# Four-layer gated transformer on one core: the 8-dim-head attentions move from bf16 stacks to fp32 slots of 64 rows, filled by copies

## What is computed

```python
scores = jnp.einsum('bqhd,bkhd->bhqk', qh, kh) / jnp.sqrt(dh)
attn = jax.nn.softmax(scores + mask, axis=-1)
ctx = jnp.einsum('bhqk,bkhd->bqhd', attn, vh)
```

## Time and profile before

| what | value |
|---|---|
| time, median of 3 executions | 2059.91 us |
| lowest, highest | 2056.92, 2062.85 us |
| the profiled execution | 2044.2 us |
| its span | 2042.4 us |
| mean granted TensorE clock | 0.862 |
| instructions | 34774 |
| busy PE, DVE, ACT, POOL | 1367.1, 1399.3, 806.4, 450.7 us |

### The profile page before, as it was taken

The page is one execution under the profiler, slowest core; times in us unless marked ns, Lnnn a source line. Parts: engine busy times, 40 slices in busy tenths (PEclk is TensorE's granted clock), DMA queues, the critical chain, the costliest instruction groups (busy, mean ns, idle before and its releaser), DMA issues. The chain is left out here.

```text
span 2042.4 us, 34774 instructions
## 1 busy us (share of the span) xinstructions
PE 1367.1 (67%) x13754; PEld 958.2 (47%) x13754; DVE 1399.3 (69%) x2126; ACT 806.4 (39%) x1151; POOL 450.7 (22%) x598
## 2 busy tenths in 40 slices
PE   0788169999999933888888731588323777130898
PEld 0465146666666621565565511466213444120797
DVE  5566447777777767677767688466685775859565
ACT  0466137776677731333333220366220676010110
POOL 6421342222222100222222103332004230000221
PEclk9999669999999976999999855699766799555898
DMA  2011322222222201000000000000000000110242
GB/s 67 1 10 10 93 63 86 87 90 87 82 92 87 87 31 33 1 1 1 1 1 1 1 11 23 1 2 2 11 10 21 1 2 1 61 21 0 88 142 87
DMA packets 97737, 76.52 MB, mean 37 GB/s; under 512 B 42612, under 2 KB 84148, under 8 KB 96692
## 3 DMA queue, kind: packets, MB, share of 16 engines
q1 hardware_dynamic: 96564, 73.10, 12.0%
q0 software_dynamic: 1024, 1.32, 0.3%
HBM read 33.10 MB, written 3.15 MB: 18 GB/s over the span
## 5 line engine op out<-in xcount | busy, mean ns | idle before, releaser
L1088 DVE TENSOR_REDUCE Mf<-bank 128x4 f32<-128x1024 f32 x192 | 234.5, 1221 | 107.4 <-PE bank L974 107.4
L551 ACT ACTIVATE Pt<-bank 128x768 f32<-128x768 f32 (+1 forms) x192 | 169.4, 882 | 135.5 <-PE bank L492 134.8
L1041 ACT ACTIVATE Pt<-bank 128x1024 f32<-128x1024 f32 x192 | 196.9, 1025 | 50.8 <-PE bank L992 50.3
L1314 POOL TENSOR_TENSOR Psum<-Pt 128x512 f32<-128x512 f32 x64 | 81.1, 1267 | 313.7 <-ACT Pt L1433 313.7
L761 PE MATMUL bank<-ident,Qf 128*128 128x128 f32 x64 | 14.3, 416 | 159.5 <-SPq L262 96.1
L1481 DVE RECIPROCAL st<-bank 128x256 f32<-128x256 f32 x64 | 111.9, 1748 | 6.5 <-PE bank L1394 6.4
L992 PE MATMUL bank<-QK 50*128 50x256 f32 x768 | 97.6, 333 | 19.4 <-DMA QK<-NMrow 19.0
L576 DVE TENSOR_REDUCE Mx<-bank 128x2 f32<-128x256 f32 x128 | 54.3, 424 | 81.6 <-PE bank L479 77.6
L1456 DVE TENSOR_TENSOR qk_lo<-bank,qk_hi 128x512 fp32r<-128x512 f32 x64 | 44.1, 689 | 95.6 <-ACT qk_hi L1425 95.6
L898 POOL CAST parts<-nodes 128x256 fp32r<-128x256 f32 x96 | 38.2, 397 | 304.7 <-PE bank L954 304.7
L1005 PE MATMUL bank<-Pt,V 128*32 128x256 f32 x1536 | 103.5, 387 | 0.1
(11 more groups left out here) (367 smaller groups left out, 3691.9 us busy)
## 6 DMA issues: line engine op xcount, KB each, us to landing
QK<-Z SPq DMA_DIRECT2D x288, 128.0 KB, 3.1
Wup<-in_L_upT SPq DMA_DIRECT2D x16, 512.0 KB, 3.5
Wdn<-in_L_downT SPq DMA_DIRECT2D x16, 256.0 KB, 3.7
Aup<-in_L_aupT SPq DMA_DIRECT2D x16, 128.0 KB, 3.5
QK<-NMrow SPq DMA_DIRECT2D x96, 4.0 KB
WeT<-in_L_WeT SPq DMA_DIRECT2D x1, 1280.0 KB
s_rows<-XG SPq DMA_DIRECT2D x1, 1032.0 KB, 7.9
tA<-in_x_heads SPq DMA_DIRECT2D x1, 1024.0 KB
```

The costliest lines, as they stand in the source:

```text
L551: act.activation(Pp[:, g % 4, :, 0:w], banks[:, 2:4, 0:w], ACT.Exp, scale=L.scale).then_inc(exp_done, 1)
L1041: act.activation(Pp[:, g % 4], banks[:, 2:4, :], ACT.Exp, scale=L.scale).then_inc(exp_done, 1)
L1088: d.tensor_reduce(m, banks[:, 0:2, :].rearrange("p h (t k) -> p h t k", t=2), AX, ALU.max).then_inc(max_done, 1)
L1314: e.tensor_tensor(Psum[:, q % 2], Pp[:, q % 4, :, 0:S], Pp[:, q % 4, :, S:2 * S], ALU.add).then_inc(key_sum, 1)
```

## The change

The class `Heads` and its functions for each engine are removed, and l0x, l2x and l3x become a `Flow` as well. A slot has 64 rows in all of them, of which A uses 63 and B all 64. The three copies of a row stand at a distance of 64/dh rows (8 for dh 8, 4 for dh 16) where l0f had 3. Row 3 of a slot (`PAD`) takes the padding mask, row 63 (`TOP`) the negated maximum. The ring of `QK` has 4 places in l0f and 3 in the others, which need 8 blocks of two slots where l0f needs 4.

What a batch of the three attentions does for its slots now, in the order of the letters in `events()`: **S**, POOL permutes q and k into `order` with four copies (L379), PE turns them with four fp32 transposes (L468), ACT copies the bank into `Z`; **L**, DVE subtracts (L653); **D**, six DMAs of 128 KB (L368) on SP, and one more in l2x for the padding mask; **N** twice per batch, two small transposes each (L514), `NMrow` (L641) and a DMA of 8 KB (L355). A is L505, B is L528, V is L545, R is L554. Masks, exp and the order A, B, V stay as they were in these attentions; l0f keeps its own order, B before A.

Around it: the blank rows are now filled by POOL for the queries (`queries_blank`, L336) and by ACT for the keys (`keys_blank`), in l0f too, where POOL had all eight; ones are written into V (`values_ones`) at each attention, and V is cleared in l0x alone; `padf` becomes `padr`, 16 by 2048, computed on POOL (L1583).

```diff
-class Heads:
-    ...
-        def att_pool(g, L, base, pad=None, early=False):
...
-                e.tensor_copy(C[:, :, 5:6], k)
-                g.link(e.tensor_copy(C[:, :, 0:4:3], wide(k, 2)))
-                g.link(e.tensor_tensor(rk, k, C[:, :, 0:1], ALU.subtract))
...
+SLOT, PAD, TOP = 64, 3, 63
...
+        self.blocks = self.H // 2
+        self.half = self.blocks // 2
+        self.step = SLOT // dh
+        self.copies = 6 + padded
+        self.ring = 4 if node else 3
...
-                if ok(b):
+                if ok(b) and self.node:
                     out.append(("B", b, j))
                 if ok(a):
                     out.append(("A", a, j))
+                if ok(b) and not self.node:
+                    out.append(("B", b, j))
...
+                elif not self.node and j == 0 and ok(w):
+                    out.append(("L", w, 0))
...
+                elif not self.node and j in (1, 3) and ok(w):
+                    out.append(("D", w, j // 2))
...
+        def queries_blank(g, L):
+            for r in range(L.ring):
+                g.eng.tensor_copy(L.QK[:, r, :, 0, :], bc(L.rowk[:, 0:1].unsqueeze(1), [P, L.blocks, S]))
+        def keys_blank(a, L):
+            for r in range(L.ring):
+                a.eng.copy(L.QK[:, r, :, 1, :], bc(L.rowk[:, 1:2].unsqueeze(1), [P, L.blocks, S]))
...
+                    if L.padded and j == 0:
+                        e.dma_start(L.QK[PAD:P:SLOT, u % L.ring, :, 1, :].bitcast(F32),
+                                    padr[:, u, :].bitcast(F32)).then_inc(L.slots_in[u % L.ring], 16)
+                    rows = slice(SLOT * j, SLOT * (j + 1))
                     for f, pick in enumerate((slice(1, 3), slice(1, 4, 2), slice(0, 3, 2))):
-                        o = L.slot * j + f
-                        e.dma_start(QK[o:o + 3 * L.dh:3, u % L.ring].bitcast(F32),
-                                    Z[rows, u % 2, pick, :].bitcast(F32)).then_inc(slots_in[u % L.ring], 16)
+                        e.dma_start(L.QK[SLOT * j + f:SLOT * (j + 1):L.step, u % L.ring].bitcast(F32),
+                                    L.Z[rows, u % 2, pick, :].bitcast(F32)).then_inc(L.slots_in[u % L.ring], 16)
...
+                if kind == "S" and not L.node:
+                    for k, src in enumerate((Qf, Kf)):
+                        for t in range(2):
+                            e.tensor_copy(L.permuted(L.order[:, u % 2, k, t, :], out=True),
+                                          L.permuted(src[:, 2 * u + t, :])).then_inc(L.parts_in, 1)
...
+                    if L.causal:
+                        mask_a(g)
+                        after, m, o = events[i + 1]
+                        if after == "B":
+                            mask_b(Pb + L.pairs * m + o)
...
+                            rs = slice(SLOT * x, SLOT * x + TOP)
+                            last = pe.matmul(bank[x][:, t * S:t * S + w],
+                                             L.QK[rs, u % L.ring, j, 0, t * P:(t + 1) * P],
+                                             L.QK[rs, u % L.ring, j, 1, 0:w], start=(not L.causal and t == 0),
+                                             stop=True, skip_group_check=True)
...
+                    else:
+                        last = act.copy(L.Z[:, u % 2, 1:3, :].rearrange("p k s -> p (k s)"), b)
...
+                    else:
+                        last = d.tensor_tensor(L.Z[:, u % 2, 0:4:3, :], b.rearrange("p (k s) -> p k s", k=2),
+                                               L.Z[:, u % 2, 1:3, :].bitcast(F32), ALU.subtract)
```

More of the change, by code:

```diff
@@ L145, in events @@
                         out.append(("O", b, 0))
-                if j == 1 and ok(z):
+                if j == (1 if self.node else self.pairs - 1) and ok(z):
                     out.append(("S", z, 0))
@@ L192, in flamingo @@
         Mx = sb("Mx", [P, 2, 16])
+        L0 = Flow("l0x", 8, True, B)
+        L0f = Flow("l0f", 16, False, 6 * B, node=True)
+        L2 = Flow("l2x", 8, True, B, padded=True)
+        L3 = Flow("l3x", 8, False, B)
+        attentions = [L0, L0f, L2, L3]
         Rden = sb("Rden", [P, 2, 16])
@@ L402, in att_steps @@
[L402 to L409 removed]
+        bases, pb_, ub_ = [], 0, 0
+        for L in attentions:
+            bases.append({"P": pb_, "U": ub_})
+            pb_, ub_ = pb_ + L.units * L.pairs, ub_ + L.units * L.outs
+        t_full, t_done, u_full, u_done = sem("t_full"), sem("t_done"), sem("u_full"), sem("u_done")
+        y_full, y_done = sem("y_full"), sem("y_done")
+        wd_in, w_full, w_hi, w_done = sem("wd_in"), sem("w_full"), sem("w_hi"), sem("w_done")
@@ L532, in turn_bank @@
[L532 to L547 removed]
+                    b = turning(kind, u, j)
@@ L548, in att_act, with flow_act @@
+        def flow_act(a, L, base):
+            act = a.eng
+            Pb, Ub = base["P"], base["U"]
+            place = L.banks()
+            for kind, u, j in L.events():
+                g = Pb + L.pairs * u + j
+                c, n = u // B, u % B
+                if kind == "B":
                     act.wait_ge(st_full, g + 1)
@@ L573, in att_dve, with flow_dve @@
+        def flow_dve(v, L, base):
+            d = v.eng
+            Pb, Ub = base["P"], base["U"]
+            place = L.banks()
+            for kind, u, j in L.events():
+                g = Pb + L.pairs * u + j
+                c, n = u // B, u % B
+                if kind == "A":
                     d.wait_ge(sm_full, g + 1)
-                    hs = slice(2 * i, 2 * i + 2)
+                    m = L.Mf[:, u % 2, j // L.half, :, 0:2 * L.half].rearrange("p t (r i) -> p r t i", r=2)
+                    m = m[:, :, :, j % L.half]
```

854 lines of the change are left out of this document (300 added, 554 removed).

## The result

| kernel | median | lowest, highest | runs |
|---|---|---|---|
| before | 2061.05 us | 2054.68, 2069.89 | 20 |
| changed | 2067.59 us | 2058.61, 2087.04 | 20 |

The ratio is 1.0038 with a 95% interval of [1.0021, 1.0055]: the change makes the kernel slower by about 8 us (the two medians lie 6.5 us apart). Measured once more on another occasion it was 1.0040 [1.0016, 1.0063]. The profiled execution took 2071.8 us, its span 2069.8. The profiled execution of before (2044.2) was an unusually short one: none of the 20 runs reached it, and another profile of the same kernel has a span of 2058.2.

A forecast was written before the change was run, and what follows sets the result against it. No engine is full; chains (rings of DVE maxima and PE scores, plus turns) bound it. Terms -20 +1.2 +3.1 +5.5 -4.2 +1.0 +0.7 +2.4 = -10.3 from 2044.2 give 2033.9, scaled to 2049.5 us; range 2032 to 2071.

The forecast's parts named there:

- An l3x batch is 15.4: Steady l3x batch: 8 x 1.81 + 0.9 us instead of 17.26; over 7 batches -13 us.
- A causal batch is 17.4: Steady batch in l0x and l2x: 8 x 2.11 + 0.5 us instead of 17.9; 7 batches, two stages, -7 us.
- +0.10 a pair: Added time per steady pair for fp32 scores on the ring, taking one of two doubled weight loads as exposed.
- +0.16, the upper bound: Highest fp32 score price per steady pair (0.50 against 0.34 us); part of the gain-eaten rival, 2060 us, chance 0.17.
- Starts, forecast +1.2: New start chains summing to 12 us each: l0x +2.8, l2x +2.4, l3x -4.0 us.
- the sign of being wrong that I had named: At the starts: the forecast would be wrong if the 8-partition copies landed in much more than 3 us.
- l2x, l3x ... +1.0 (bounds 0 and +6): Preparations: three POOL fills of 2.1 us each, ones for V and the padding row lie at barriers, +1.0 us.
- +0.7 for ACT's fills before l3x: Preparation of l3x: ACT's fills there add 0.7 us.
- +3.1 and +5.5: First batches: fp32 scores at 1.2 GHz cost 3.1 us; the clock rising two or three pairs later costs 5.5, three stages.
- my third rival: Slower by the clock: 1.2 GHz lasts a further batch with both kinds in each stage, +20 us, 2070; chance 0.18.
- l0f, -4.2: Fills before l0f: POOL writes 4 of 8, about 1.04 us each, serial up to the barrier, so 4.2 us saved.
- Tails, +2.4: Ends with only transposed scores left: ring of exp and scores, 8 pairs per stage at +0.1 us, 2.4 us in all.

The follow-up runs named there:

- e4: Changed kernel with the causal scores of the first 128 queries computed for 256 keys instead of 128: 2065.44 us, ratio 1.0041 to the kernel before.
- e2: Changed kernel with six 128 KB copies into 8 partitions made three of 256 KB into 16: 2058.26 us, ratio 1.0007 to the kernel before.
- e6: Changed kernel with 64 unused PE matmuls during the wait for the first copies, none behind the first batch's scores: 2071.25 us, ratio 1.0049 to before.
- e11: e10 with the transposed scores B one pair earlier in l0x, l2x and l3x, as in the kernel before: 2018.87 us, ratio 0.9797 to before.
- e10: Changed kernel with padding row on ACT, 16-partition copies, busy PE (40 start matmuls instead of 64), ACT filling l0x's query blanks: 2022.09 us, ratio 0.9831 to before.
- e7: Kernel before with extra unused PE matmuls at the starts and behind first-batch scores of l0x, l2x and l3x: 2047.02 us, ratio 0.9940.
- e9: Kernel before with one unused POOL TENSOR_TENSOR at the beginning of l3x's preparation: 2050.79 us, ratio 0.9964.

## Why the prediction was wrong, point by point

The median lies in the stated range, but I forecast 10 us less and got about 8 us more: the sign is wrong. The two largest errors are the starts (8 us) and the preparation of l2x (6 us).

- **Steady batches.** "An l3x batch is 15.4": measured 15.08, so this large gain came as said, 12.3 us from first to last maximum. "A causal batch is 17.4": 17.63. The term mis-sized is the +0.10 a pair; +0.16, the upper bound, was right for causal pairs, which fits what e4 shows. It took about half of the 7 us that I had entered for both causal stages.
- **Starts, forecast +1.2, measured +9.3: this step failed.** The chain up to the copies was nearly right (from POOL's first copy to the first issue 4.8 us in l2x, 4.2 by my terms). The copies were not. I read l0f's 7.06 us as the time of 12 copies and took 7.1 to 8.6 "at worst" for six; but the row's 12 issues are six of the first unit and six of the second, and the first scores wait for six. So 7.06 was already the time of six, into 16 partitions, and no ceiling. Into 8 partitions they needed 9.7 in l2x, and landed 5.8 us after the last issue, which is the sign of being wrong that I had named ("much more than 3 us"). l3x got -2.0 instead of -4.0, l0x and l2x +5.6 and +5.7 instead of +2.8 and +2.4. I had the rule that speaks against this and left it out of the forecast; the size that I worked out from it, 1 us a start, was a quarter of what e2 gave back.
- **"l2x, l3x ... +1.0 (bounds 0 and +6)": this step failed too.** The preparation of l2x became 7 us longer, outside my bounds, and that of l3x stayed (35.0 in both). I priced three fills by l0f's row and passed over the padding row as something that lies at a barrier, though the kernel before showed 6.75 us of issue ahead of the same operation (L1793, 0.32 us there), and a 16x2048 operation has 128 times the elements a partition of the 128x16 one before. With the starts and this step as forecast the sum would have been about -3 instead of +11. The +0.7 for ACT's fills before l3x did not show.
- **The low clock.** In the causal stages place and sign were right: +3.1 and +5.5 were forecast for all three, and their first two batches are 5.4 us longer together. In l3x the first batch became 1.2 us shorter where I had added 1.3. That the rest of PE in the start causes it, as the term of +5.5 and my third rival assumed, is refuted by e6; the fear of that rival, a whole further batch at 1.2 GHz, did not come true in full: the second batch is 2 to 3 us longer than a later one.
- **l0f, -4.2.** The fills took 9.58 us and now go side by side on two engines:

```profile
258.35 3.88 ACT L341 CAST l0f_QK<-l0f_rowk 128x1024 fp32r<-128x1024 f32 x4 [2.40 <-DMA V<-in_L_ffn_We]
258.45 4.81 POOL L336 CAST l0f_QK<-l0f_rowk 128x1024 fp32r<-128x1024 f32 x4 [13.06 <-DMA V<-in_L_ffn_We]
```

  4.81 us on POOL: -4.8. The whole stretch from l0x's last exp to l0f's first maximum is 6.4 us shorter. Another 1.4 of it are l0f's first six copies, ready 7.0 to 7.1 us after the first issue in the four profiles on the basis of before and 5.6 to 5.8 in five of the changed kernel and its variants. Their rows now stand 4 apart instead of 3; whether that is the reason, no run tells.
- **Tails, +2.4, measured +6.1.** I priced products where the order was most of the cause: e11 gives back 5.2 of the 6.1. The order stood in the diff: B of a pair was ahead by one before.
- **Left out altogether:** +3.2 in the preparation of l0x (the idle time of 6.74 us ahead of POOL's rotation; e10).

The measured terms add up to 3.2 + 9.3 + (2.0 + 2.4 - 12.3) + 6.1 - 6.4 + 7 = +11 us. The second profile of before and that of the changed kernel differ by 11.6, the medians by 6.5, and the ratio says 8. The 3 to 5 us between the sum and the last two are of the size by which the untouched stretches scatter, and I have no run that assigns them.

## What to carry to other kernels

When work moves to another form, price what it does at the barriers as carefully as the loop: here the loops gained 8 us and starts, preparations and ends lost 19. For a copy into few partitions no row of a wider copy is a ceiling; join copies until they span as many partitions as they can. And look at the first and last batch of a pipeline by themselves: they had a clock and an order of their own. Mended in all this, the changed kernel is 2% faster than the one before, though that one would gain from two of the repairs as well (e7 and e9, 12 and 7 us, not run together).
